# Softmax sums added up in the first key tile's buffer, one pool of eight PSUM banks, and weight splits shared between ScalarE and GpSimd

## The chip, the cores and the metric

The kernel is one launch on one core of a Trainium2 chip. The metric is device microseconds of one execution. Five engines have queues of their own and meet through semaphores: TensorE (PE in the profile, its weight loads PEld), VectorE (DVE), ScalarE (ACT), GpSimd (POOL) and SyncE (SP, which only issues DMAs). A wait stands in an engine's queue, so that everything behind a waiting instruction waits too.

## The reference, cut to what matters

Two layers over x of shape (2, 1024, 128), each with a residual:

```python
x = x + layernorm(attention(layernorm(x)))
x = x + layernorm(experts(layernorm(x)))

# attention: 8 query heads, 2 key heads (4 query heads each), causal
q = x @ wq
k = (x @ wk_down) @ wk_up
v = (x @ wv_down) @ wv_up
probs = softmax(mask(q k^T / sqrt(128)))      # exp / sum of exp
y = (probs @ v) @ wo

# experts: 32 routed (6 taken per token), one shared, 16 anchors (1 taken)
eo = (silu(x @ w_gate) * (x @ w_up)) @ w_down
```

## The kernel before, in words

**Tiling.** The 2048 rows are four chunks of 512 (two per batch). Attention runs over eight blocks n = 0 to 7, each one chunk of queries and one key head with its four query heads. Blocks 0, 1, 6 and 7 have four key tiles of 128 keys, blocks 2 to 5 have eight. Keys past the diagonal are left out, so the last four tiles of a block are 512, 384, 256 and 128 query columns wide.

**A block's steps.** `p1` (L1333, with the mask at L1336) multiplies queries by keys, and VectorE takes each row's maximum (`max`, L1095). The maxima, transposed (L1343), go by DMA into the rows below the queries. `p2` (L1354, mask L1356) multiplies again, the other way round and with the maximum subtracted, and ScalarE writes the exponentials of one key tile (four heads, 128x512 each) into `probs` (`exp`, L940), a ring of four buffers. `pv` (L1368) multiplies them by the values into the fixed PSUM bank `acc`. For the softmax's denominator, GpSimd adds each odd key tile into the even one before it, in two instructions of two heads (`add`, L759); `ones` (L1378) then multiplies the even tile by a column of ones, into the fixed PSUM bank `total`, once per pair of tiles. VectorE turns `total` into a reciprocal (`recip`, L1112 to L1114) and scales `acc` by it (`yl`, L1121). The `p1` of block n + 1 is laid between the `p2` of block n.

**After attention** each chunk goes through a projection (`post_out`, L1388), two normalisations and the routing, and then through 21 tiles of expert weights: three products `g` and three `u` (L1240 to L1242: each fp32 product is three products of rounded parts, high by high, low by high and high by low), `silu` (L971), a product with the routing weight on GpSimd (`mul`, L839), `h` (L1167), its high and low parts `hi` (L981) and `lo` (L1172), and `down` (L1439 to L1441) into the bank `acc`.

**The expert weights** are split into the same two parts during attention, in 22 pieces of at most 128x384: GpSimd writes the high part (L785, L790) and subtracts it (L786, L791).

**The order.** A planner (`Order.settle`) simulates the engines with the costs and ranks that `plan` gives each step, always starting the step that can start first (by rank if several can), and so writes every engine's queue and deals out six rotating PSUM banks. The order is fixed before the launch; on the chip only semaphores decide when each instruction starts. `bank_turn` makes TensorE wait until the bank's last reader is done.

Of the kernel before, what the change touches and what calls it, by code (L numbers as in the profile page):

```python
# [13 lines left out]
P = 128  # L14
# [34 lines left out]
BANKS = 6  # L49
KTBUF = 4  # L50
QRING = 3
HRING = 3
WSPLITS = range(0, MT, 3)
# [58 lines left out]
def halves_of(ev):  # L112

    return {j // 2 for j in range(ev[3], ev[3] + ev[4])}
# [5 lines left out]
ROUTE_RANK = (5.5, 100, 121, 142)  # L120
# [80 lines left out]
def plan():  # L201
# [7 lines left out]

    step("SP", ("x_load",), 320, 0)  # L210
# [5 lines left out]
    step("PE", ("warm",), 560, 0)  # L216
# [18 lines left out]
    step("PE", ("hold",), 130, 0.5, ("xT", 0))  # L235
# [33 lines left out]
    for n in range(NB):  # L269
# [25 lines left out]
        for x, ev in enumerate(steps):  # L295
# [5 lines left out]
            old = KT[n, kt] - KTBUF  # L301
            done = None
            if old >= 0:
                on, okt = KT_AT[old]
                done = ("ones", on, okt) if okt % 2 == 0 else ("add", on, okt, 1)
            step("ACT", ("exp", *ev[1:]), 22 + w * own * 80 // 1000, rank, ev, old >= 0 and ("pv", *KT_AT[old]), done)
            if ev == [e for e in steps if e[2] == kt][-1]:
                exps = [("exp", *e[1:]) for e in steps if e[2] == kt]
                step("PE", ("pv", n, kt), 10 + cols * 17 // 100, rank - 0.2, *exps, *vs,
                     ("pv", n, kt - 1) if kt else n >= 1 and ("yl", n - 1))  # L310
# [6 lines left out]
        step("DVE", ("recip", n), 170, n + 2, ("ones", n, kts(n) - 2))  # L317
# [30 lines left out]
    for a in range(3):  # L348
        step("SP", ("load", a), 200, 2, ("s_dma", 0) if a == 0 else ("wsplit", a - 1, WSPLITS[-1]))
        for t in WSPLITS:  # L350
            step("POOL", ("wsplit", a, t), 155, 3 + 2 * a + t / MT, ("wsplit", a, t - 3) if t else ("load", a), ("k_dma", NCH - 1) if a == 2 and t == 0 else None)

    last_exp = ("exp", *p2_steps(NB - 1)[-1][1:])
    for k in range(NU):
        m, t = divmod(k, MT)
        rank = 100 + k
        need = [("post_T_lo", m)] + ([("wsplit", 2, WSPLITS[-1]), last_exp] if k == 0 else [])
        if t != SHARED:
            step("PE", ("g", k), 68, rank, *need, k >= 1 and (("g", k - 1) if (k - 1) % MT != SHARED else ("u", k - 1)), bank=1, until=("silu", k))
# [22 lines left out]
    for half in range(2):  # L382
        step("ACT", ("tail_copy", half), 38, rank, ("down", NU - 1), ("fin_T", NCH - 2), half and ("tail_copy", 0))
        step("PE", ("tail_T", half), 27, rank, ("tail_copy", half), ("yl", NB - 1), bank=1 - half, until=("tail_center", half))
# [8 lines left out]
KT_AT = [(n, kt) for n in range(NB) for kt in range(kts(n))]  # L393
KT = {at: k for k, at in enumerate(KT_AT)}
# [28 lines left out]
ADD = count("POOL", "add")  # L423
MUL = count("POOL", "mul")
WSPLIT = count("POOL", "wsplit")
# [11 lines left out]
def build(nc, x, wq, small, wo, gate_bias, w_gate, w_up, w_down,  # L437
          shared_w_gate, shared_w_up, shared_w_down, anchor_w_gate, anchor_w_up, anchor_w_down, out):
    with ExitStack() as ctx:
# [94 lines left out]
        acc = ctx.enter_context(nc.psum_tensor("acc", [P, CH], F32))  # L534
        total = ctx.enter_context(nc.psum_tensor("total", [P, CH], F32))
# [57 lines left out]
        added = sem("added")  # L593
# [3 lines left out]
        route_done = sem("route_done")  # L597
        split_done = sem("split_done")
# [23 lines left out]
        def _(sp):  # L622
# [6 lines left out]
            for ev in PLAN["SP"]:  # L629
# [7 lines left out]
                elif kind == "load":  # L637
# [50 lines left out]
        def _(pool):  # L688
# [13 lines left out]
            for ev in PLAN["POOL"]:  # L702
# [805 lines left out]
```

## Time and profile before

| | |
|---|---|
| median of 3 runs | 416.88 us (416.11 to 418.38) |
| the profiled execution's own time | 416.28 us |
| its span in the trace | 414.2 us (2.1 us lie around it) |
| mean granted TensorE clock | 0.986 |
| TensorE matmul busy | 393.9 us, 95% of the span |
| VectorE busy | 281.5 us, 68% |
| GpSimd busy | 275.7 us, 67% |
| ScalarE busy | 231.4 us, 56% |

A matmul's busy time is modelled and overlaps with that of its neighbours, so what a matmul costs TensorE is read from the distance between starts, not from its duration. Attention proper lies between about 48 and 222 us of the span, the experts from there to 403 us, the tail behind.

### The profile page before, as it was taken

The page shows a single profiled execution, that of the slowest core. Times are in us where ns is not written, and L with a number is a line of the kernel's source. Part 1 is how long each engine was busy: PE and PEld are TensorE (multiplying, and loading weights), DVE is VectorE, ACT ScalarE, POOL GpSimd, SP SyncE. Part 2 cuts the span into 40 slices and gives each one's busy share as a digit, 9 for nine tenths or more (in the row PEclk, how much of TensorE's full clock was granted, in tenths as well). Part 3 has the DMA queues.
Part 4 walks back from the last instruction along what each step waited for, and adds up shares of the span by engine and source line. Part 5 has one row for each costly group of instructions (what it writes and reads, how often), then busy time and mean ns, then how long its engine had stood idle before and what let it go on. Part 6 is the DMA issues. An engine that isn't in the chain of part 4 may idle for free.

```text
span 414.2 us, 7003 instructions
## 1 busy us (share of the span) xinstructions
PE 393.9 (95%) x2168; PEld 260.5 (63%) x2168; DVE 281.5 (68%) x711; ACT 231.4 (56%) x450; POOL 275.7 (67%) x338
## 2 busy tenths in 40 slices
PE   8998999998999999999998999999999999999993
PEld 8664555553454644444556778767887788778871
DVE  5985897882857885526347776678765686557665
ACT  4555355564545466664675455865556655665643
POOL 6124867975976498473667886498963988477651
PEclk9989999998999999999999999999999999999997
DMA  7347090083230050500000000001000000000000
GB/s 215 52 108 169 16 220 13 0 196 52 40 38 3 2 77 3 71 9 2 3 0 2 1 1 2 0 0 28 1 1 2 25 2 0 1 2 25 0 2 25
DMA packets 9906, 14.56 MB, mean 35 GB/s; under 512 B 1232, under 2 KB 5520, under 8 KB 9488
## 3 DMA queue, kind: packets, MB, share of 16 engines
q1 hardware_dynamic: 9584, 13.49, 15.7%
q10 hardware_dynamic: 288, 0.64, 0.5%
q8 instruction: 19, 0.31, 0.4%
q14 instruction: 15, 0.12, 0.1%
HBM read 6.26 MB, written 1.05 MB: 18 GB/s over the span
## 4 chain that ended last, share of the span: by engine, by line
PE 77%; POOL 7%; DVE 6%; ACT 4%; issue 3%; DMA 2%; SPq 1%; POOLq 0%; DVEq 0%; ACTq 0%
PE ps L1240 9%; PE ps L1242 9%; PE ps L1241 9%; PE ps L1354 9%; PE ps L1333 9%; PE acc L1368 8%; PE total L1378 5%; PE acc L1439 4%; PE acc L1441 4%; PE acc L1440 4%; POOL silu L839 3%; DMA qst<-q_lo 2%; PE ps L1336 2%; PE ps L1356 1%; PE ps L1388 1%
## 5 line engine op out<-in xcount | busy, mean ns | idle before, releaser
L839 POOL TENSOR_TENSOR silu<-silu,cwb 128x512 f32<-128x512 f32 x80 | 102.5, 1292 | 40.3 <-ACT silu L971 35.8
L1095 DVE TENSOR_REDUCE nmax_h<-ps 128x1 f32<-128x512 f32 (+3 forms) x152 | 92.3, 655 | 47.8 <-PE ps L1336 24.3
L940 ACT ACTIVATE probs<-ps 128x512 f32<-128x512 f32 (+1 forms) x152 | 80.0, 579 | 70.2 <-PE ps L1354 43.7
L759 POOL TENSOR_TENSOR probs<-probs 128x768 f32<-128x768 f32 (+2 forms) x48 | 78.0, 1644 | 34.0 <-ACT probs L940 21.2
L1172 DVE TENSOR_TENSOR h_lo<-ps,h_hi 128x512 fp32r<-128x512 f32 (+1 forms) x84 | 57.0, 686 | 23.8 <-ACT h_hi L981 23.2
L1167 DVE TENSOR_TENSOR ps<-silu,ps 128x512 f32<-128x512 f32 (+1 forms) x84 | 57.9, 693 | 22.3 <-POOL silu L839 17.5
L971 ACT ACTIVATE silu<-ps 128x512 f32<-128x512 f32 x80 | 47.5, 597 | 45.5 <-PE ps L1242 39.7
L1333 PE MATMUL ps<-kst,qst 96*128 96x512 f32 (+3 forms) x192 | 63.8, 386 | 4.0 <-ACT probs L940 1.9
L1240 PE MATMUL ps<-xT_hi,w_hi 128*128 128x512 f32 x164 | 65.4, 399 | 1.3 <-ACT silu L971 1.3
L1242 PE MATMUL ps<-xT_hi,w_lo 128*128 128x512 f32 x164 | 64.4, 393 | 0.0
L1241 PE MATMUL ps<-xT_lo,w_hi 128*128 128x512 f32 x164 | 64.4, 393 | 0.0
L1354 PE MATMUL ps<-qst,kst 98*128 98x512 f32 (+1 forms) x152 | 62.4, 445 | 1.9 <-ACT probs L940 1.4
L981 ACT ACTIVATE h_hi<-ps 128x512 fp32r<-128x512 f32 (+1 forms) x84 | 49.8, 596 | 21.9 <-DVE ps L1167 20.9
L1333 PEld LDWEIGHTS ps<-kst,qst 96*128 96x128 f32 x192 | 34.0, 191 | 26.2 <-issue 21.1
L1354 PEld LDWEIGHTS ps<-qst,kst 98*128 98x128 f32 x152 | 27.9, 192 | 24.5 <-issue 21.9
L1368 PE MATMUL acc<-probs,v_sb 128*32 128x512 f32 (+3 forms) x384 | 40.4, 507 | 1.3 <-DVE ylat L1121 0.5
L1240 PEld LDWEIGHTS ps<-xT_hi,w_hi 128*128 128x128 f32 x164 | 30.8, 188 | 11.6 <-ACT silu L971 2.5
L1439 PE MATMUL acc<-h_hi,wd_hi 128*128 128x512 f32 (+1 forms) x84 | 35.0, 417 | 2.5 <-DVE h_lo L1172 2.4
L1242 PEld LDWEIGHTS ps<-xT_hi,w_lo 128*128 128x128 f32 x164 | 30.8, 188 | 6.8
L1241 PEld LDWEIGHTS ps<-xT_lo,w_hi 128*128 128x128 f32 x164 | 30.8, 188 | 6.7
L1441 PE MATMUL acc<-h_hi,wd_lo 128*128 128x512 f32 (+1 forms) x84 | 33.2, 395 | 0.0
L1440 PE MATMUL acc<-h_lo,wd_hi 128*128 128x512 f32 (+1 forms) x84 | 33.2, 395 | 0.0
(191 smaller groups left out, 518.7 us busy)
## 6 DMA issues: line engine op xcount, KB each, us to landing
qst<-q_hi SPq DMA_DIRECT2D x14, 256.0 KB, 5.6
qst<-q_lo SPq DMA_DIRECT2D x7, 256.0 KB, 6.1
x_sb<-in_attn_x SPq DMA_DIRECT2D x4, 256.0 KB, 6.5
raw<-in_ffn_w_gate SPq DMA_DIRECT2D x1, 1024.0 KB, 4.9
raw<-in_ffn_w_up SPq DMA_DIRECT2D x1, 1024.0 KB, 6.4
raw<-in_ffn_w_down SPq DMA_DIRECT2D x1, 1024.0 KB, 5.0
kst<-k_hi SPq DMA_DIRECT2D x6, 128.0 KB, 3.7
result<-x_sb SPq DMA_DIRECT2D x3, 256.0 KB, 2.3
```

What stands on the lines that cost most here:

```text
L759: nc.gpsimd.tensor_tensor(into, into, probs[:, k % KTBUF, js, cols], ALU.add).then_inc(added, 1)
L839: nc.gpsimd.tensor_tensor(silu[:, k % HRING, :], silu[:, k % HRING, :], cwb[:, m % 2, t // ET, :], ALU.mult).then_inc(scaled_ready, 1)
L940: nc.scalar.activation(probs[:, k % KTBUF, j:j + w, at:at + cols], bank(full)[:, 0:w * cols].rearrange("p (w c) -> p w c", w=w), ACT.Exp). ...
L1095: nc.vector.tensor_reduce(nmax_h[:, n % 2, i, j:j + w, h], bank(full)[:, 0:w * keys].rearrange("p (w k) -> p w k", w=w), AX.X, ALU.max, ne ...
L1167: nc.vector.tensor_tensor(up, silu[0:rows, k % HRING, :], up, ALU.mult).then_inc(h_ready, 1)
L1172: nc.vector.tensor_tensor(h_lo[0:rows, k % HRING, :], bank(("u", k))[0:rows], h_hi[0:rows, k % HRING, :].bitcast(F32), ALU.subtract).then_ ...
L1240: nc.tensor.matmul(dst, lhs[0], rhs[0], start=True, stop=False)
L1241: nc.tensor.matmul(dst, lhs[0], rhs[1], start=False, stop=False)
L1242: return nc.tensor.matmul(dst, lhs[1], rhs[0], start=False, stop=True)
L1333: last = nc.tensor.matmul(s[:, r, :], qst[0:QROWS, n % QRING, j + r, P * i:P * i + P], kst[0:QROWS, g, at:at + keys], start=(r == 0), stop ...
L1354: last = nc.tensor.matmul(s, kst[0:KROWS, g, at:at + P], qst[0:KROWS, n % QRING, j:j + w, first:first + cols], start=True, stop=not masked)
L1368: last = nc.tensor.matmul(acc[LAT * j:LAT * j + LAT, cols], v_sb[:, (T // P) * b + kt, LAT * g:LAT * g + LAT], probs[:, KT[n, kt] % KTBUF, ...
```

## The change

**Denominator.** All key tiles of a block are now added into the buffer of its first tile (kt = 0), one after the other, and `ones` runs once per block, at its end. An `add` is two instructions side by side: GpSimd takes the first two or three heads and VectorE the rest (`SPLIT`). So a block of eight tiles has seven adds on each of the two engines where GpSimd had four tiles' worth in eight instructions. The first tile's buffer is held to the end of the block, and three buffers rotate.

**Banks.** `acc` and `total` are gone. All eight PSUM banks rotate, and `pv`, `ones`, `down`, the warm-up products and the tail take theirs from the pool.

**Weights.** ScalarE writes the high parts (`whi`), GpSimd only subtracts. The down weights go from the last tiles to the first, because the first tiles of `wd_hi` lie over `k_hi` and `k_lo`, from which the last k transfer reads: only those wait for it.

**Transition.** The experts' buffers lie over `probs`. `silu`, `hi` and `lo` of the first three tiles now wait only for the reads of the one `probs` buffer under them (`rows_left`), instead of for all `pv` and `ones`.

```diff
-BANKS = 6
+BANKS = 8
 KTBUF = 4
+ADDERS = ("POOL", "DVE")
+SPLIT = (2, 3, 3, 3, 3, 3, 2, 2)
-WSPLITS = range(0, MT, 3)
+WSPLITS = [list(range(0, MT, 3)), list(range(0, MT, 3)), list(range(0, MT, 3))[::-1]]
+OVER_K = 2 * CH // P
-ROUTE_RANK = (5.5, 100, 121, 142)
+ROUTE_RANK = (5.5, 98, 121, 142)
...
+def part_heads(n, part):
+    return (SPLIT[n], REP) if part else (0, SPLIT[n])
...
-            step("ACT", ("exp", *ev[1:]), 22 + w * own * 80 // 1000, rank, ev, old >= 0 and ("pv", *KT_AT[old]), done)
+            step("ACT", ("exp", *ev[1:]), 22 + w * own * 80 // 1000, rank, ev, *leaves(WAS[n, kt]))
...
-                if kt % 2:
-                    for half in range(2):
-                        step("POOL", ("add", n, kt, half), 2 * (8 + cols * 252 // 1000), rank - 0.1, ("pv", n, kt - 1),
-                             *[e for e in exps if half in halves_of(e)])
-                    step("PE", ("ones", n, kt - 1), 10 + (CH - first_col(n, kt - 1)) * 17 // 100, rank - 0.2, ("add", n, kt, 0), ("add", n, kt, 1),
-                     ("ones", n, kt - 3) if kt > 1 else n >= 1 and ("recip", n - 1))
+                for part, engine in enumerate(ADDERS):
+                    if kt:
+                        j, end = part_heads(n, part)
+                        cost = 18 + (end - j) * cols * 215 // 1000 if engine == "POOL" else 15 + (end - j) * cols * 105 // 1000
+                        step(engine, ("add", n, kt, part), cost, rank - 0.1, ("pv", n, 0), *[e for e in exps if part in parts_of(e)], kt > 1 and ("add", n, kt - 1, part))
+        step("PE", ("ones", n), 10 + CH * 17 // 100, n + 2.9, *(("add", n, kts(n) - 1, part) for part in range(len(ADDERS))), bank=1, until=("recip", n))
...
+            step("ACT", ("whi", a, t), 55, 3 + 2 * a + i / len(WSPLITS[a]), ("load", a), i and ("whi", a, WSPLITS[a][i - 1]), a == 2 and t < OVER_K and ("k_dma", NCH - 1))
+            step("POOL", ("wsplit", a, t), 103, 3 + 2 * a + i / len(WSPLITS[a]), ("whi", a, t), before)
...
+        def rows_left(engine, row):
+            kt = (1, 2, 3, 0)[row // REP]
+            engine.wait_ge(pv_done, PV["pv", NB - 1, kt])
+            for part in range(len(ADDERS)):
+                engine.wait_ge(added[part], ADD[part]["add", NB - 1, kt, part])
...
+                elif kind == "add":
+                    _, n, kt, part = ev
+                    j, end = part_heads(n, part)
+                    cols = slice(first_col(n, kt), CH)
+                    into = probs[:, BUF[n, 0], j:end, cols]
+                    dve.wait_ge(pv_done, PV["pv", n, 0])
+                    dve.wait_ge(exp_ready, max(EXP["exp", *e[1:]] for e in p2_steps(n) if e[2] == kt and part in parts_of(e)))
+                    if kt > 1:
+                        dve.wait_ge(added[part], ADD[part]["add", n, kt - 1, part])
+                    nc.vector.tensor_tensor(into, into, probs[:, BUF[n, kt], j:end, cols], ALU.add).then_inc(added[part], 1)
```

Two places show how the queues move. VectorE before, in the `p1` of block 4, with block 3 being added up on GpSimd (L1095 is `max`, L1089 and L1081 are low parts of a projection and of a transposed chunk):

```order
L1121 TENSOR_TENSOR ylat<-acc,rb 128x512
L1095 TENSOR_REDUCE nmax_h<-ps 128x1
L1095 TENSOR_REDUCE nmax_h<-ps 128x2
L1089 TENSOR_TENSOR q_lo<-ps,q_hi 128x512
L1095 TENSOR_REDUCE nmax_h<-ps 128x2
L1095 TENSOR_REDUCE nmax_h<-ps 128x1 x9
L1081 TENSOR_TENSOR xT_lo<-ps,xT_hi 128x512
L1095 TENSOR_REDUCE nmax_h<-ps 128x1 x4
```

VectorE at the same place in the changed kernel (L1143 is `max`, L1137 and L1129 the same low parts, L1166 the `add` of one head):

```order
L1179 TENSOR_TENSOR ylat<-ps,rb 128x512
L1143 TENSOR_REDUCE nmax_h<-ps 128x2
L1137 TENSOR_TENSOR q_lo<-ps,q_hi 128x512
L1143 TENSOR_REDUCE nmax_h<-ps 128x2
L1166 TENSOR_TENSOR probs<-probs 128x512
L1143 TENSOR_REDUCE nmax_h<-ps 128x1 x3
L1166 TENSOR_TENSOR probs<-probs 128x512
L1143 TENSOR_REDUCE nmax_h<-ps 128x1 x6
L1129 TENSOR_TENSOR xT_lo<-ps,xT_hi 128x512
L1166 TENSOR_TENSOR probs<-probs 128x512
L1143 TENSOR_REDUCE nmax_h<-ps 128x1 x6
```

The adds stand among the maxima, one per key tile: three to six maxima lie between two of them. TensorE before, at the end of block 3 (L1368 is `pv`, L1333 and L1336 are `p1` of block 5, L1378 is `ones`):

```order
L1333 MATMUL ps<-kst,qst 128x512 x2
L1368 MATMUL acc<-probs,v_sb 32x256 x4
L1368 MATMUL acc<-probs,v_sb 32x128 x4
L1333 MATMUL ps<-kst,qst 128x128 x4
L1336 MATMUL ps<-mask,ident_bf 128x512
L1378 MATMUL total<-probs,ones 32x512 x4
L1378 MATMUL total<-probs,ones 32x256 x4
```

TensorE at the same place in the changed kernel (L1435 is `pv`, L1401 and L1404 are `p1` of block 5, L1422 is `p2` of block 4):

```order
L1401 MATMUL ps<-kst,qst 128x512 x2
L1435 MATMUL ps<-probs,v_sb 32x256 x4
L1435 MATMUL ps<-probs,v_sb 32x128 x4
L1401 MATMUL ps<-kst,qst 128x128 x4
L1404 MATMUL ps<-mask,ident_bf 128x512
L1422 MATMUL ps<-qst,kst 128x512 x2
```

Both `ones` groups are gone from here, and the block's single one stands eight rows further on, among the `p2` of block 4. Over the whole queue there are 8 groups of `ones` instead of 24 (16 of 512 columns and 8 of 256).

## Rows read from the trace of the kernel before

**Rows 1.** The page, parts 1 and 2: busy times, forty slices of the span.

```profile
PE 393.9 (95%) x2168; PEld 260.5 (63%) x2168; DVE 281.5 (68%) x711; ACT 231.4 (56%) x450; POOL 275.7 (67%) x338
...
PEclk9989999998999999999999999999999999999997
```

**Rows 2.** Busy time by stage: stretch, its length, each engine's busy us (instructions), clock.

```profile
48.50:222.50 174.00, 169.04 (x1090) 87.16 (x1091) 113.27 (x286) 97.50 (x195) 121.12 (x133) 0.99 0.24 44
222.50:403.40 180.90, 177.80 (x791) 140.74 (x789) 126.39 (x313) 106.96 (x201) 132.12 (x159) 1.00 0.02 5
```

**Rows 3.** The same by block, PE, PEld, DVE, ACT, POOL: blocks 1 to 5.

```profile
48.50:72.70 24.20, 23.13 (x135) 12.75 (x135) 21.09 (x40) 12.04 (x24) 17.73 (x23) 1.00 0.49 105
72.70:110.50 37.80, 35.91 (x218) 18.92 (x218) 24.84 (x56) 19.66 (x42) 29.39 (x33) 0.95 0.32 68
110.50:139.10 28.60, 28.14 (x182) 13.64 (x182) 20.27 (x54) 14.88 (x29) 20.49 (x23) 1.00 0.20 29
139.10:172.30 33.20, 32.43 (x207) 16.72 (x206) 23.71 (x74) 21.95 (x47) 22.47 (x27) 1.00 0.20 33
172.30:194.60 22.30, 22.21 (x157) 10.02 (x157) 9.80 (x18) 11.57 (x24) 14.39 (x8) 1.00 0.22 27
```

**Rows 4.** Waits: who waited for whom, us in total, times, longest.

```profile
DVE nmax_h L1095 <- PE ps L1336: 24.3, 19, 3.5
DVE nmax_h L1095 <- PE ps L1333: 23.1, 17, 5.3
```

**Rows 5.** Timeline, TensorE alone, around two `ones` groups: start, duration, instruction.

```profile
216.07 0.39 PE L1241 MATMUL ps<-xT_lo,w_hi 128*128 128x512 f32 x1
216.30 0.40 PE L1242 MATMUL ps<-xT_hi,w_lo 128*128 128x512 f32 x1
216.63 1.06 PE L1378 MATMUL total<-probs,ones 128*32 128x512 f32 x8
217.62 0.50 PE L1240 MATMUL ps<-xT_hi,w_hi 128*128 128x512 f32 x1
217.96 0.39 PE L1241 MATMUL ps<-xT_lo,w_hi 128*128 128x512 f32 x1
218.19 0.40 PE L1242 MATMUL ps<-xT_hi,w_lo 128*128 128x512 f32 x1
218.52 0.64 PE L1378 MATMUL total<-probs,ones 128*32 128x256 f32 x8
219.09 0.50 PE L1240 MATMUL ps<-xT_hi,w_hi 128*128 128x512 f32 x1
219.42 0.39 PE L1241 MATMUL ps<-xT_lo,w_hi 128*128 128x512 f32 x1
```

**Rows 6.** Groups by form: GpSimd's adds, a ScalarE exponential; busy us, mean ns, idle before.

```profile
L759 POOL TENSOR_TENSOR probs<-probs 128x1024 f32<-128x1024 f32 x16 | 37.8, 2378 | 8.2 <-PE acc L1368 6.6 <-ACT probs L940 1.6
L759 POOL TENSOR_TENSOR probs<-probs 128x256 f32<-128x256 f32 x16 | 11.3, 729 | 4.2 <-PE acc L1368 4.2
L940 ACT ACTIVATE probs<-ps 128x384 f32<-128x384 f32 x32 | 14.8, 491 | 9.0 <-PE ps L1354 8.7
```

**Rows 7.** Groups by line: GpSimd's high parts of the weights.

```profile
L785 POOL CAST w_hi<-raw 128x384 fp32r<-128x384 f32 (+1 forms) x14 | 6.9, 494 | 1.9 <-DMA raw<-in_ffn_anchor_w_up 1.9
L790 POOL CAST wd_hi<-raw 128x384 fp32r<-128x384 f32 (+2 forms) x8 | 3.7, 459 | 6.9 <-DMA kst<-k_lo 6.9
```

**Rows 8.** Page, part 5: a VectorE instruction with two inputs, one in PSUM.

```profile
L1172 DVE TENSOR_TENSOR h_lo<-ps,h_hi 128x512 fp32r<-128x512 f32 (+1 forms) x84 | 57.0, 686 | 23.8 <-ACT h_hi L981 23.2
```

**Rows 9.** The four instructions of line 1142: shortest, median and longest ns.

```profile
L1142 DVE TENSOR_TENSOR ties<-gscore x4: 216/217/1308, 129.7 to 322.4; 128x64 f32<-128x64 f32 x4
```

**Rows 10.** Timeline, VectorE and GpSimd, where both read SBUF.

```profile
276.60 1.29 POOL L839 TENSOR_TENSOR silu<-silu,cwb 128x512 f32<-128x512 f32 x1
277.10 0.87 DVE L1141 TENSOR_TENSOR above<-gscore 128x64 f32<-128x64 f32 x1
277.85 1.27 POOL L767 TENSOR_TENSOR x_sb<-x_sb,normed_x 128x512 f32<-128x512 f32 x1
277.89 1.31 DVE L1142 TENSOR_TENSOR ties<-gscore 128x64 f32<-128x64 f32 x1
```

**Rows 11.** Timeline around the transition; in brackets the idle time ahead.

```profile
219.26 1.28 ACT L971 ACT_TABLE_LOAD   x1 [3.04 <-PE total L1378]
...
221.20 0.50 PE L1240 MATMUL ps<-xT_hi,w_hi 128*128 128x512 f32 x1 [0.46 <-ACT silu L971]
```

**Rows 12.** Page, part 5: TensorE's two products of scores, with their idle time.

```profile
L1333 PE MATMUL ps<-kst,qst 96*128 96x512 f32 (+3 forms) x192 | 63.8, 386 | 4.0 <-ACT probs L940 1.9
...
L1354 PE MATMUL ps<-qst,kst 98*128 98x512 f32 (+1 forms) x152 | 62.4, 445 | 1.9 <-ACT probs L940 1.4
```

More of the change, by code:

```diff
@@ L109, in p2_steps, with parts_of, buffers @@
     return out
-def halves_of(ev):
-    return {j // 2 for j in range(ev[3], ev[3] + ev[4])}
+def part_heads(n, part):
+    return (SPLIT[n], REP) if part else (0, SPLIT[n])
+def parts_of(ev):
+    return {part for part in range(len(ADDERS)) if ev[3] < part_heads(ev[1], part)[1] and part_heads(ev[1], part)[0] < ev[3] + ev[4]}
+def buffers():
+    held, at, was = [None] * KTBUF, {}, {}
+    turn = list(range(KTBUF))
+    for n in range(NB):
+        for kt in range(kts(n)):
+            own = turn.pop(0)
+            if kt == 0:
+                first = own
+            else:
+                turn.append(own)
+            at[n, kt], was[n, kt], held[own] = own, held[own], (n, kt)
+        turn.append(first)
+    name = {at[NB - 1, kt]: k for k, kt in enumerate((1, 2, 3, 0))}
+    return {x: name[own] for x, own in at.items()}, was
 WARM = 14
@@ L208, in chunk_of, with leaves @@
         return CPB * b + c
+    def leaves(user, parts=range(len(ADDERS))):
+        if user is None:
+            return []
+        n, kt = user
+        return [("pv", n, kt), *(("add", n, kt, part) for part in parts)] if kt else [("ones", n)]
     step("SP", ("x_load",), 320, 0)
@@ L390, in plan @@
     return o, o.settle()
-KT_AT = [(n, kt) for n in range(NB) for kt in range(kts(n))]
-KT = {at: k for k, at in enumerate(KT_AT)}
+BUF, WAS = buffers()
 PLACED, PLAN = plan()
@@ L422 @@
 RSTD = count("POOL", "xn_rstd", "post_rstd", "post_rstd2", "fin_rstd")
-ADD = count("POOL", "add")
+ADD = [{ev: k + 1 for k, ev in enumerate(e for e in PLAN[engine] if e[0] == "add" and e[3] == part)} for part, engine in enumerate(ADDERS)]
 MUL = count("POOL", "mul")
-WSPLIT = count("POOL", "wsplit")
+W_HI = count("ACT", "whi")
 LN = {ev: k for k, ev in enumerate(MOM)}
@@ L592, in build @@
         pv_done = sem("pv_done")
-        added = sem("added")
+        added = [sem(f"added{part}") for part in range(len(ADDERS))]
         ones_done = sem("ones_done")
@@ L1371, in _ @@
                 elif kind == "ones":
-                    _, n, kt = ev
-                    cols = slice(first_col(n, kt), CH)
-                    pe.wait_ge(added, max(ADD["add", n, kt + 1, part] for part in range(2)))
-                    if kt == 0 and n >= 1:
-                        pe.wait_ge(recip_ready, n)
+                    n = ev[1]
+                    for part in range(len(ADDERS)):
+                        pe.wait_ge(added[part], ADD[part]["add", n, kts(n) - 1, part])
+                    bank_turn(ev)
                     for j in range(REP):
-                        last = nc.tensor.matmul(total[LAT * j:LAT * j + LAT, cols], ones[:], probs[:, KT[n, kt] % KTBUF, j, cols],
-                                                start=(kt == 0), stop=(kt == kts(n) - 2))
+                        last = nc.tensor.matmul(bank(ev)[LAT * j:LAT * j + LAT, :], ones[:], probs[:, BUF[n, 0], j, :], start=True, stop=True)
                     last.then_inc(ones_done, 1)
@@ L1418, in _ @@
                     if k == 0:
-                        pe.wait_ge(split_done, 3 * len(WSPLITS))
+                        pe.wait_ge(split_done, sum(len(order) for order in WSPLITS))
                     bank_turn(ev)
```

168 lines of the change are left out of this document (87 added, 81 removed).

## The prediction

> **What bounds the kernel now.** I read the page first, then the busy time by stage, then by block, then single instructions where a stage gains or loses. On the page TensorE is busy for 95% of the span, VectorE for 68%, GpSimd for 67%, ScalarE for 56% [rows 1]. By stage: TensorE is busy for 169.0 of the 174.0 us of attention and for 177.8 of the 180.9 us of the experts [rows 2]. So TensorE sets the pace in both, the experts' products are not touched, and the change can win or lose only in attention and at the seam behind it. By block the second engine is close: VectorE is busy for 21.1 of 24.2 us in block 1, and for 24.8 of 37.8, 20.3 of 28.6 and 23.7 of 33.2 us in blocks 2 to 4; GpSimd for 29.4, 20.5 and 22.5 us there [rows 3]. VectorE's free time is mostly a wait for scores from TensorE, 24.3 + 23.1 us over the span [rows 4]. That is what I expect to matter: the change takes work off the first engine and puts it on the second and the third.
>
> **What goes: `ones`.** The cost to TensorE is read from starts, since matmuls overlap. From the start of the L1242 product at 216.30 to that of the L1241 at 217.96 are 1.66 us; two steps between such products without `ones` are 2 x 0.23 (216.07 to 216.30); so a group of 512 columns costs 1.20 us. In the same way 218.19 to 219.42 is 1.23, less 0.46, gives 0.77 us for 256 columns [rows 5]. Before there are 16 wide and 8 narrow groups, after it 8 wide: 8 x 1.20 + 8 x 0.77 = 15.8 us less for TensorE, 3.2 us in each block of eight key tiles (3 x 1.20 + 0.77 - 1.20) and 0.8 in each of the four short ones.
>
> **What is added on GpSimd.** Its adds take 2378 ns for 1024 columns and 729 for 256 [rows 6]: 2.15 ns per column and 0.18 us. Three heads of 512 columns are then an estimated 3.48 us, and a long block (four tiles of 512 columns, then 384, 256, 128) costs 4 x 3.48 + 2.65 + 1.83 + 1.00 = 19.4 us, where it now costs 4 x 2.38 + 2 x 1.82 + 2 x 0.73 = 14.6: 4.8 us more. The short blocks fall slightly or stay. The high parts of the weights leave it, 6.9 + 3.7 = 10.6 us in all [rows 7], some 2 us of it in each of blocks 2 and 3.
>
> **What is added on ScalarE.** 22 copies of up to 128x384, by the 384-column exponential's 0.49 us [rows 6] 10.8 us, beside its 97.5 busy of 174 [rows 2]: nothing. A copy that waits for a weight load now holds the exponentials behind it, and TensorE's `pv` behind those. GpSimd waited 1.9 us for w_up and 6.9 for the k transfer ahead of the down weights [rows 4, 7]; the reversed order puts the tiles that do not need the transfer first. I take 0, with 5 us as the upper end (6.9 less the 1.9 that lie beside other work).
>
> **What is added on VectorE.** No SBUF-to-SBUF add of this size is in the trace. Between the 0.69 us of a 512-column subtraction with one input in PSUM [rows 8] and the 0.217 us median of 64 columns with both in SBUF [rows 9] lie 1.05 ns per column. So a long block costs 4 x 0.69 + 0.55 + 0.42 + 0.28 = 4.0 us, a short one at most 2.1.
>
> **The two adders in each other's way.** This is the term that decides. At 277.10 VectorE starts L1141, 64 columns with both inputs in SBUF, while GpSimd's product runs from 276.60 to 277.89. It takes 0.87 us and ends at 277.97. The next, L1142, starts at 277.89, GpSimd's L767 runs from 277.85 to 279.12, and it takes 1.31 us, to 279.20 [rows 10]. The median of the same instruction is 0.217 us [rows 9]. Each time VectorE ended 0.08 us behind GpSimd: it stood until the other had finished. GpSimd lost nothing (1.27 and 1.29 us). The new adds are just such instructions, on both engines at once.
>
> The Trainium skill says the same against this change (SBUF — State Buffer, Who interferes with whom): a VectorE instruction with two SBUF inputs takes its second through the read port that GpSimd uses, and whichever starts second stands until the first has ended, however long that is. The trace agrees, by those two rows. Without the rule and the rows the sum would be the 400 us of the second rival.
>
> How long is such a wait? GpSimd's adds in a long block have a mean remaining time, at a random moment in one, of (4 x 3.48² + 2.65² + 1.83² + 1.00²) / (2 x 19.4) = 1.55 us. GpSimd's needs in blocks 2 to 5 are 32.2, 23.3, 27.3 and 19.2 us (its busy time [rows 3], 4.8 more each, 2 less in the first two), 102 in all: 93% of the 109 us that TensorE would need there, 78% of the 131 that the sum below comes to. I take 85%, so 1.3 us per add and 9.1 per long block. From below it is 0. From above, VectorE's add becomes ready a head's exponential (0.6 us) after GpSimd's has started, and waits 2.5 us on the four wide tiles and 1 us on the others, 13 us per block.
>
> **The sum, block by block.** The longest of the three needs sets a block. VectorE's need is its busy time [rows 3] + 4.0 + 9.1.
>
> Block 2: VectorE 37.9 against TensorE 37.8 - 3.2 = 34.6; now 37.8, so +0.1. Block 3: VectorE 33.4 against 25.4; now 28.6, so +4.8. Block 4: VectorE 36.8 against 30.0; now 33.2, so +3.6. Block 5: VectorE 22.9; GpSimd 14.4 + 4.8 + 2.8 (its own turn behind seven VectorE adds) = 22.0; TensorE 19.1; now 22.3, so +0.6. Together +9.1.
>
> Block 1: VectorE 21.1 + 1.3 + three short waits, 1.2, is 23.6 against TensorE's 23.4; now 24.2, so -0.6. Blocks 0, 6 and 7 keep TensorE's -0.8 each, -2.4. At the seam ScalarE waited 3.04 us for the last `ones` before it loaded the table for silu, and TensorE then 0.46 us for silu [rows 11]; with the waits per buffer I take -1. The eight banks and the ranks: both products of scores together have 5.9 us of idle time ahead of them, most of it not for maxima [rows 12], so more banks are worth nothing here.
>
> Sum: 9.1 - 0.6 - 2.4 - 1 = +5.1 us on the profiled execution's 416.28, so 421.4, where the median of its runs is 416.88. I predict 421.
>
> **Bounds.** With no wait between the adders: block 2 to 4 by TensorE (-9.6), block 5 by GpSimd's 19.2 (-3.1), the others -4.2: 399.4. With the upper wait: VectorE 41.8, 37.3, 40.7 and 26.8 gives +24.7, the others -4.0: 437.0.
>
> **Rivals.**
> First, the waits are real but lie in time that VectorE has anyway. For it: 47.4 us of VectorE's idle time are waits for scores [rows 4], and in the sparse stretches behind a block's last maximum an add can stand without anyone waiting. Against it: VectorE's adds stand three to six maxima apart amid the `p1` of the next block, where TensorE needs the banks that the maxima free. If 0.5 us of each wait counts (3.5 per long block), VectorE's needs are 32.3, 27.8 and 31.2, so TensorE keeps block 2 (-3.2), and blocks 3 and 4 give -0.8 and -2.0, block 5 is -0.3 by GpSimd: with the -4.0, -10.3, so 406. I give 404 to 414 a chance of 0.29.
>
> Second, TensorE keeps the whole gain, as by its own work alone, the lower bound: 399 to 404. For it: TensorE is at 97% in attention [rows 2]. Against it: the waits of [rows 10]. Chance 0.09.
>
> Third, the worse side of my own mechanism: VectorE's add always comes just behind GpSimd's, and GpSimd itself, near full in blocks 3 to 5, delays the single `ones` at the block's end. It decides from about 2 us per wide add: above 429, up to 437. Chance 0.11.
>
> Fourth, gain and wait cancel, between 415 and 419. For it: both are of the same size, 15.8 against 9.1 per long block less VectorE's free time. Chance 0.13.
>
> That the change does not do what it says is excluded for `ones`: the queue has 8 groups. For the order of the down weights the price is the 0 to 5 us above.
>
> **How the numbers follow.** My forecast, VectorE bound by the waits at 419 to 429, has 0.38. A run of this kernel is told from no change at about 0.5%, 2.1 us. Slower: 0.38 + 0.11 = 0.49. Same: 0.13. Faster: 0.29 + 0.09 = 0.38. The range of 8 in 10 leaves out the lowest and the highest tenth: 404 to 431. The forecast's own range is 419 to 429.
>
> **What would show it.** TensorE's `ones` line: 64 records for 192, about 8 us of busy time for 21.9. VectorE's adds of 512 columns: a mean near 2 us, where 0.69 would refute the wait; GpSimd's 1536-column add near 3.5 us. VectorE's waits for scores should shrink from 47 us to under 20, and TensorE should wait in blocks 2 to 4 for maxima (`nmax_h`), which it hardly does now [rows 12]. Blocks 3 and 4 should be longer than 28.6 and 33.2 us, the experts' 181 us unchanged. I am wrong if the VectorE adds run at 0.7 us, or if they take 2 us and blocks 2 to 4 are still shorter than before.

## The result, and the profile after

The changed kernel takes 442.38 us (median of 4 runs, 439.23 to 445.77), where the kernel before took 416.5 beside it (415.19 to 418.38). The ratio is 1.062, with a 95% interval of 1.053 to 1.071. The forecast of 421 had the sign right. The time lies 11 us above the top of its range. The profiled execution took 442.87 us, 440.8 of them its span.

The page after, parts 1 and 2, answers to [rows 1]:

```profile
PE 402.0 (91%) x2040; PEld 267.2 (61%) x2040; DVE 352.7 (80%) x751; ACT 241.3 (55%) x472; POOL 288.5 (65%) x308
...
PEclk9999979898986596989699999999999999999999
```

VectorE is 71 us busier. TensorE runs 128 records fewer and is 8 us busier all the same: the clock row has holes in attention where it had none to speak of before, and the records last longer at the lower clock (blocks 1 to 5 under `reduce`: 158.3 for 135.7 us with the same 819). The experts are as before: from 267 to 430 us TensorE is busy for 161.2 of 163.0.

The blocks after, answering to [rows 3], blocks 1 to 5 and then 6 and 7 (stretch, length, PE, PEld, DVE, ACT, POOL, granted clock, DMA):

```profile
44.60:72.00 27.40, 24.61 (x125) 14.14 (x124) 24.88 (x41) 12.61 (x26) 14.11 (x12) 0.88 0.43 94
72.00:115.40 43.40, 37.04 (x204) 20.27 (x205) 40.02 (x66) 25.43 (x54) 31.06 (x23) 0.92 0.28 59
115.40:158.50 43.10, 36.90 (x168) 18.57 (x167) 38.16 (x60) 16.64 (x31) 22.03 (x11) 0.72 0.13 19
158.50:196.80 38.30, 32.76 (x176) 16.86 (x176) 35.83 (x57) 18.53 (x36) 26.68 (x22) 0.87 0.24 35
196.80:227.10 30.30, 27.01 (x151) 12.11 (x151) 25.81 (x51) 15.75 (x32) 23.73 (x15) 0.89 0.08 11
227.10:238.00 10.90, 10.50 (x76) 5.96 (x74) 7.77 (x21) 6.42 (x16) 6.96 (x11) 1.00 0.01 3
238.00:249.50 11.50, 10.65 (x76) 6.02 (x76) 8.96 (x33) 7.96 (x16) 8.26 (x11) 1.00 0.00 1
```

A block ends where VectorE scales its `pv` (`yl`). Blocks 1 to 5 are 3.4, 5.6, 14.5, 5.1 and 8.0 us longer than before (by the same ends of blocks: 24.0, 37.8, 28.6, 33.2, 22.3). Blocks 0, 6 and 7 are 3.4, 4.2 and 1.3 shorter. That makes 27.7 by the end of the last block, and the span is 26.6 longer. Block 5 also holds 33 VectorE instructions more than before (51 for 18): its seven adds, six maxima more (block 6 has seven fewer), and some 20 short ones, mostly of the routing, that ran in block 4 before.

The adds and `ones` after, by form (busy us, mean ns, idle before), answering to [rows 6]:

```profile
L807 POOL TENSOR_TENSOR probs<-probs 128x1536 f32<-128x1536 f32 x16 | 56.4, 3522 | 26.0 <-ACT probs L987 19.4 <-issue 4.3 <-PE ps L1435 2.0
L1166 DVE TENSOR_TENSOR probs<-probs 128x512 f32<-128x512 f32 x19 | 46.7, 2460 | 1.2 <-ACT probs L987 0.6 <-issue 0.4
...
L1444 PE MATMUL ps<-probs,ones 128*32 128x512 f32 x64 | 8.8, 619 | 1.0 <-POOL probs L807 0.8 <-DVE nmax_h L1143 0.2
```

VectorE's wide add takes 2460 ns, where 512 columns with one input in PSUM take 693. One of them, with GpSimd beside it, answering to [rows 10]:

```profile
78.48 3.82 DVE L1166 TENSOR_TENSOR probs<-probs 128x512 f32<-128x512 f32 x1
...
78.29 3.46 POOL L807 TENSOR_TENSOR probs<-probs 128x1536 f32<-128x1536 f32 x1
```

GpSimd's ends at 81.75, VectorE's at 82.30: it stood for 3.3 us and ran on for 0.55 us. At 104.17 GpSimd is idle, and an add of 384 columns takes 0.54. So what one add costs hangs on where GpSimd is when it comes.

The waits (who waited for whom, us in total, times, longest), answering to [rows 4]:

```profile
PE ps L1401 <- DVE nmax_h L1143: 9.0, 9, 2.1
...
DVE nmax_h L1143 <- PE ps L1404: 5.8, 10, 2.4
DVE nmax_h L1143 <- PE ps L1401: 5.5, 9, 1.9
PE ps L1422 <- DVE nmax_h L1143: 5.1, 3, 2.4
```

They have turned round: VectorE waited 47.4 us for scores, now 11.3, and TensorE waits 14.1 us for maxima.

### The profile page after: what moved, and what is told of

It reads as the page before. It is cut to its first block, busy times and chain, and to the rows that moved or that the text cites. A ratio compares the mean times of both kernels' runs of the same rounds, so it can differ in the third digit from the quotient of the medians.

```text
span 440.8 us, 6951 instructions
## 1 busy us (share of the span) xinstructions
PE 402.0 (91%) x2040; PEld 267.2 (61%) x2040; DVE 352.7 (80%) x751; ACT 241.3 (55%) x472; POOL 288.5 (65%) x308
## 4 chain that ended last, share of the span: by engine, by line
PE 45%; DVE 8%; POOL 3%; issue 3%; ACT 2%; POOLq 0%; ACTq 0%; DVEq 0%
PE ps L1308 8%; PE ps L1309 8%; PE ps L1310 8%; PE ps L1502 5%; PE ps L1504 4%; PE ps L1503 4%; DVE probs L1166 2%; PE ps L1422 2%; DVE nmax_h L1143 2%; PE ps L1435 2%; PE ps L1401 2%; POOL probs L807 1%; ACT probs L987 1%; POOL silu L874 1%; DVE h_lo L1232 1%
## 5 line engine op out<-in xcount | busy, mean ns | idle before, releaser
L807 POOL TENSOR_TENSOR probs<-probs 128x1536 f32<-128x1536 f32 (+5 forms) x40 | 97.7, 2444 | 60.9 <-ACT probs L987 45.3
L1143 DVE TENSOR_REDUCE nmax_h<-ps 128x1 f32<-128x512 f32 (+3 forms) x152 | 92.2, 650 | 11.4 <-PE ps L1404 5.8
L1401 PE MATMUL ps<-kst,qst 96*128 96x512 f32 (+3 forms) x192 | 71.4, 431 | 12.4 <-DVE nmax_h L1143 9.0
L1422 PE MATMUL ps<-qst,kst 98*128 98x512 f32 (+1 forms) x152 | 68.5, 487 | 6.5 <-DVE nmax_h L1143 5.1
L1166 DVE TENSOR_TENSOR probs<-probs 128x512 f32<-128x512 f32 (+4 forms) x40 | 67.5, 1688 | 5.2 <-ACT probs L987 3.1
L1017 ACT ACTIVATE silu<-ps 128x512 f32<-128x512 f32 x80 | 47.4, 597 | 43.2 <-PE ps L1310 37.7
L1401 PEld LDWEIGHTS ps<-kst,qst 96*128 96x128 f32 x192 | 39.3, 219 | 32.6 <-issue 27.9
L1422 PEld LDWEIGHTS ps<-qst,kst 98*128 98x128 f32 x152 | 31.3, 215 | 32.4 <-issue 30.5
L1435 PE MATMUL ps<-probs,v_sb 128*32 128x512 f32 (+3 forms) x384 | 46.1, 567 | 0.5 <-ACT probs L987 0.5
L1502 PE MATMUL ps<-h_hi,wd_hi 128*128 128x512 f32 (+1 forms) x84 | 34.7, 414 | 3.3 <-DVE h_lo L1232 3.2
L1503 PE MATMUL ps<-h_lo,wd_hi 128*128 128x512 f32 (+1 forms) x84 | 33.2, 395 | 0.0
```

The source lines that it names most:

```text
L807: nc.gpsimd.tensor_tensor(into, into, probs[:, BUF[n, kt], j:end, cols], ALU.add).then_inc(added[part], 1)
L1143: nc.vector.tensor_reduce(nmax_h[:, n % 2, i, j:j + w, h], bank(full)[:, 0:w * keys].rearrange("p (w k) -> p w k", w=w), AX.X, ALU.max, ne ...
L1166: nc.vector.tensor_tensor(into, into, probs[:, BUF[n, kt], j:end, cols], ALU.add).then_inc(added[part], 1)
L1401: last = nc.tensor.matmul(s[:, r, :], qst[0:QROWS, n % QRING, j + r, P * i:P * i + P], kst[0:QROWS, g, at:at + keys], start=(r == 0), stop ...
L1422: last = nc.tensor.matmul(s, kst[0:KROWS, g, at:at + P], qst[0:KROWS, n % QRING, j:j + w, first:first + cols], start=True, stop=not masked)
```

## The experiments

All of them start from the changed kernel. Theory A: VectorE's adds stand behind GpSimd's because both their inputs are in SBUF, and this standing is the loss. Its rivals: the adds' own work, the place in the queue or the planner's order (B), and, later, TensorE's lowered clock as a loss in its own right (C).

**reduce.**

```
- nc.vector.tensor_tensor(into, into, probs[:, BUF[n, kt], j:end, cols], ALU.add)
+ nc.vector.tensor_reduce(spare[:, kt - 1, j:end], probs[:, BUF[n, kt], j:end, cols], AX.X, ALU.max)
```

> The changed kernel, with each add on VectorE replaced by a reduction over the same heads and columns (one SBUF input; VectorE's share of the denominators is left out). Same queues, same work on VectorE, no second SBUF input. Theory A (VectorE stands while GpSimd reads SBUF, and that stop spreads to TensorE and its clock): the reductions take about 0.69 us instead of 2.46, TensorE is at the lower clock for under 15 us instead of 58, and the time is 398 to 408 us. Theory B (the 20 us of extra work on VectorE, or the held buffer and the single ones at the end of a block, are what costs): still above 430 us, with reductions at 0.69 us.

Measured: 404.53 us (403.73 to 405.18), 0.968 of the kernel before (0.964 to 0.971).

```profile
L1167 DVE TENSOR_REDUCE spare<-probs 128x1 f32<-128x512 f32 x16 | 10.9, 680 | 2.6 <-ACT probs L988 1.5 <-issue 1.2
```

The same tile, place in the queue and waits, but one SBUF input, and the instruction takes 680 ns while GpSimd adds beside it. That is 38 us off the changed kernel. B is out as an explanation of the loss. One detail missed: with a mean clock of 0.975 over 401.7 us TensorE spent an estimated 20 us at half clock, where under 15 were expected. Its blocks 1 to 5:

```profile
44.00:66.70 22.70, 21.25 (x126) 12.07 (x126) 21.93 (x42) 12.55 (x26) 12.37 (x11) 1.00 0.48 112
66.70:105.50 38.80, 35.08 (x205) 19.31 (x205) 31.04 (x65) 25.21 (x54) 30.13 (x24) 0.91 0.33 67
105.50:132.80 27.30, 26.80 (x168) 14.18 (x168) 25.85 (x60) 16.30 (x31) 21.25 (x11) 1.00 0.21 31
132.80:164.80 32.00, 29.30 (x176) 15.84 (x175) 26.84 (x58) 18.33 (x36) 25.45 (x21) 0.95 0.28 42
164.80:188.80 24.00, 23.31 (x151) 10.83 (x149) 19.51 (x51) 15.33 (x32) 22.57 (x17) 1.00 0.11 14
```

This is the table that gives the size. In the changed kernel VectorE is busier in these blocks by 2.9, 9.0, 12.3, 9.0 and 6.3 us, 39.5 together, and the blocks are longer by 4.7, 4.6, 15.8, 6.3 and 6.3, 37.7 together. Nearly every microsecond that VectorE is busier by is a microsecond of the kernel. Blocks 1 to 5 as one stretch, first in the changed kernel, then in `reduce`:

```profile
44.60:227.10 182.50, 158.32 (x819) 81.95 (x818) 164.70 (x271) 88.96 (x178) 117.60 (x83) 0.85 0.23 42
...
44.00:188.80 144.80, 135.73 (x819) 72.23 (x818) 125.18 (x272) 87.72 (x178) 111.76 (x82) 0.96 0.29 53
```

VectorE is idle for 17.8 us there in the one and for 19.6 in the other. The standing did not go into its idle time; it came on top.

**one_column.**

```
- nc.vector.tensor_tensor(into, into, probs[:, BUF[n, kt], j:end, cols], ALU.add)
+ few = probs[:, BUF[n, 0], j:end, CH - 1:CH]
+ nc.vector.tensor_tensor(few, few, probs[:, BUF[n, kt], j:end, CH - 1:CH], ALU.add)
```

> The changed kernel, with each add on VectorE cut to one column of its heads (the rest of VectorE's share of the denominators is left out). VectorE keeps two SBUF inputs but has hardly any work. Theory A: each such add still ends when GpSimd's instruction does, so it takes 1 to 2 us on the wide tiles in place of 0.16, and the time stays at 425 to 440 us. Theory B: the time falls to 400 to 410 us.

Measured: 428.11 us (425.83 to 429.22), 1.023 of before (1.017 to 1.028).

```profile
L1167 DVE TENSOR_TENSOR probs<-probs 128x1 f32<-128x1 f32 x31 | 44.3, 1431 | 4.1 <-ACT probs L987 4.0
```

One column with two SBUF inputs takes twice as long as 512 columns with one, and a kernel with almost no adding work on VectorE is 24 us slower than `reduce`, which reads the whole tile. So the standing costs without the work, as A says. Its blocks 1 to 5:

```profile
44.10:213.50 169.40, 149.46 (x820) 76.65 (x819) 150.33 (x272) 89.12 (x178) 112.26 (x83) 0.91 0.25 45
```

Against `reduce` VectorE is 25.2 us busier there and the blocks are 24.6 longer. But the changed kernel, where the adds stand about as long and do their work besides, is busier by another 14.4 us and longer by another 13.1. So beside the standing the work of the adds is paid as well; VectorE's idle time is again about the same, 19.1 us.

**per_head.**

```
- nc.gpsimd.tensor_tensor(into, into, probs[:, BUF[n, kt], j:end, cols], ALU.add)
+ for h in range(j, end):
+     one = probs[:, BUF[n, 0], h, cols]
+     last = nc.gpsimd.tensor_tensor(one, one, probs[:, BUF[n, kt], h, cols], ALU.add)
```

> The changed kernel, with GpSimd's add cut into one instruction per head (512 columns, 1.28 us, instead of 1536 columns, 3.52 us); VectorE unchanged, result complete. Theory A: VectorE's wait ends with GpSimd's current instruction, so its 512-column add falls from 2.46 us to 1.2 to 1.5 us, and the time to 408 to 425 us, though GpSimd issues some 8 us more. Theory B: GpSimd has more to do and the time is 442 us or more.

Measured: 425.52 us (423.81 to 425.96), 1.018 of before (1.014 to 1.022), half a microsecond above the 408 to 425 that A gave.

```profile
L1169 DVE TENSOR_TENSOR probs<-probs 128x512 f32<-128x512 f32 x19 | 21.7, 1140 | 1.5 <-issue 0.9 <-ACT probs L990 0.2
...
L1447 PE MATMUL ps<-probs,ones 128*32 128x512 f32 x64 | 11.1, 775 | 5.7 <-POOL probs L809 5.4 <-DVE nmax_h L1146 0.3
```

With GpSimd's instruction cut to a third, VectorE's wide add falls from 2460 to 1140 ns and the time by 17 us. The wait goes with the length of GpSimd's single instruction, as A says (it gave 1.2 to 1.5 us for the add). In return GpSimd is 15 us busier (303.8 for 288.5), and `ones` at the blocks' ends now waits 5.4 us for it.

**psum_sum.** VectorE has one head in every block; its sum lies in a fixed PSUM bank, seven banks rotate (and the planner's cost of the last add is 80 higher, for the copy back).

```
- SPLIT = (2, 3, 3, 3, 3, 3, 2, 2)
+ SPLIT = (3,) * 8
- BANKS = 8
+ BANKS = 7
+ if kt == 1: last = tensor_tensor(dsum[:, cols], into[:, 0, :], probs[:, BUF[n, kt], j, cols], ALU.add)
+ else:       last = tensor_tensor(dsum[:, cols], dsum[:, cols], probs[:, BUF[n, kt], j, cols], ALU.add)
+ (after the last tile)  tensor_copy(probs[:, BUF[n, 0], j, whole], dsum[:, whole])
```

> The changed kernel with VectorE's share (one head in every block) summed in a PSUM bank of its own: all its adds but the first of a block have one SBUF input, and a copy back to SBUF closes a block; seven banks rotate. Result complete. Theory A: only the 8 first adds can stand, and the time is 400 to 412 us, faster than the kernel before. Theory B: 435 us or more, since VectorE has 4 us more to do in copies.

Measured: 436.2 us (431.09 to 436.43), 1.039 of before (1.031 to 1.048): A's forecast missed by 24 us.

```profile
L1170 DVE TENSOR_TENSOR dsum<-probs 128x512 f32<-128x512 f32 x4 | 13.0, 3240 | 0.0
...
L1172 DVE TENSOR_TENSOR dsum<-dsum,probs 128x512 f32<-128x512 f32 x12 | 8.3, 692 | 1.9 <-issue 1.8
```

The mechanism holds within one kernel: with `dsum` as an input 692 ns, with both inputs in SBUF 3240. I had left one of the latter in each block, and in the four long ones it ran into a GpSimd add of 1536 columns (in the four short ones, with 384 columns, it took 1182 ns). Whether that, the bank that is gone or the new split made the rest, this run alone can't say. The next two were made to tell.

**seven_banks.** The edit is `BANKS = 8` to `7` in the changed kernel, the control.

> The changed kernel with seven PSUM banks in the rotation in place of eight, nothing else; the control for psum_sum and for filler. If the missing bank is what psum_sum paid for: 450 us or more, and the first block ends near 52 us as there. If a bank fewer is worth little: 440 to 447 us, first block ends within 2 us of the 45.3 us of the changed kernel.

Measured: 448.88 us (447.28 to 456.93), 1.079 of before (1.070 to 1.088); the same kernel again, as `seven_again`, 451.18 (447.02 to 454.11), 1.076 (1.063 to 1.089). The numbers fall between the two cases: a bank costs 6.5 us, in the second pair 8.8, and most of it is in block 0, which ends at 51.0 us (50.0) for 45.3. Blocks 2 to 5 took 151.1 and 156.5 us, for 155.1 with eight banks: there a bank fewer shows no effect. So the forecast's step "more banks are worth nothing here" was wrong: it looked at the two products of scores and not at the first block.

> The kernel of seven_banks again, on the same chip as light_filler, as the other side of that comparison: 447 to 452 us, clock near 0.936.

**psum_copy.** As `psum_sum`, the split as in the changed kernel, and no VectorE add with two SBUF inputs in blocks 1 to 5 (the planner's costs for the copies are 69 each):

```
+ if kt == 1: link(nc.vector.tensor_copy(dsum[:], probs[:, BUF[n, 0], j, :]))
+ last = nc.vector.tensor_tensor(dsum[:, cols], dsum[:, cols], probs[:, BUF[n, kt], j, cols], ALU.add)
```

> Seven banks; in the five blocks where VectorE has one head (1 to 5), the sum of that head lies in the eighth bank: the first tile is copied there by VectorE, each later tile is added with one input in PSUM and one in SBUF, and the sum is copied back to the first tile's buffer. The first, seventh and eighth block are as in the changed kernel. Result complete. No VectorE instruction there reads two SBUF inputs. Theory A (VectorE's two-SBUF-input adds stand until GpSimd's instruction ends, and this is the loss): adds 0.7 us each, time 405 to 418 us, so equal to or better than the kernel before. Rival S (psum_sum was slow for the bank or the planner's order, not for its eight first adds): 430 us or more. Copies that read one SBUF input should take 0.7 us even while GpSimd adds.

Measured: 421.39 us (417.97 to 422.53), 1.012 of before (1.003 to 1.021).

```profile
L1173 DVE TENSOR_TENSOR dsum<-dsum,probs 128x512 f32<-128x512 f32 x16 | 11.1, 695 | 1.0 <-issue 0.8
...
L1172 DVE COPY dsum<-probs 128x512 f32<-128x512 f32 x5 | 3.4, 687 | 0.2 <-issue 0.2
```

Against its own control with seven banks it is 27.5 us faster, though VectorE runs ten instructions more. It is a few microseconds over the 418 that A gave; S (430 or more) is out. Block by block against `psum_sum`, the latter's eight first adds and split cost 2.3 us in block 0, 12.3 in blocks 1 to 5 and 4.8 in blocks 6 and 7, 19.4 in all, of which 15.8 are left at the end of the span. So its miss of 24 us was mostly in my edit: some 7 us are the bank's, some 15 these two together, and how those share it was not separated.

**psum_take.** All eight banks rotate; the sum's bank is handed out with one more TensorE instruction and comes back after the copy back.

```
+ step("PE", ("take", n), 60, rank - 0.2, *exps, ("pv", n, 0), bank=1, until=("add", n, kts(n) - 1, 1))
+ nc.tensor.matmul(bank(ev), ident[:], probs[:, BUF[n, 0], SPLIT[n], :], start=True, stop=True)
```

> As psum_copy, but all eight banks rotate: in blocks 1 to 5 the bank for VectorE's sum is taken from the rotation when TensorE copies the first tile's head there (one matmul with the identity, some 0.5 us), and given back after VectorE's copy back. Result complete. Theory A, and the first block's 5 us of psum_copy being the price of the missing bank: first block ends near 45 us, blocks 3 to 5 as in psum_copy, 412 to 418 us in all, so 0 to 1.5% below the kernel before. Rival: the bank held through a block costs as much as the missing one: 420 us or more.

Measured: 414.26 us (median of 6, 407.56 to 415.76), the kernel before 416.56 (median of 11, 412.83 to 421.53). Block 0 ends at 46.0 us, and the wide add takes 692 ns. The result is complete: the change with its fault mended. The medians are 0.6% apart and the runs overlap, so it is the kernel before or a little better, and no more can be said. Its block 2 takes 42.8 us for 37.8 before, at a granted clock of 0.88; why is open.

**casts_back.** The 22 roundings of the high parts go back to GpSimd: `step("POOL", ("whi", a, t), 55, ...)` and `nc.gpsimd.tensor_copy`.

> The changed kernel with the 22 roundings of the weights' high parts given back to GpSimd (some 0.75 us a tile), ahead of its subtractions. If the moved roundings cost nothing and bring GpSimd little within attention: 440 to 447 us, as the changed kernel. If GpSimd's time in attention is what sets the blocks: 450 us or more, since 22 times 0.75 to 1.4 us come back on it. If ScalarE's copies were in the way: below 438 us.

Measured: 439.66 us (439.28 to 443.49), 1.060 of before (1.051 to 1.069), against 1.062 with them on ScalarE. The move costs and brings nothing that shows.

**filler and light_filler.** Are the holes in the clock a loss of their own? TensorE gets one more 128-column product ahead of each second product of scores, in seven banks, so against `seven_banks`.

```
+ nc.tensor.matmul(idle[:, 0:P], ident[:], ident[:], start=True, stop=True)
  pe.wait_ge(shift_in[n % QRING], 16 * (n // QRING + 1))
```

> As seven_banks, with one more 128-column matmul of the identity, into a bank that nobody reads, queued ahead of each of the 152 second score passes, before that pass's wait. It adds TensorE work (at the full clock near 0.15 us each, some 20 us in all where TensorE is the bound), and keeps TensorE active just ahead of waits. Theory C (the waits draw the clock to half, and this makes half of the loss or more): the mean granted clock comes back toward 0.97 and the time rises by less than the 20 us, or falls: between 15 us below and 8 us above seven_banks. Theory W (the waits alone make the loss, the clock is a small part): time up by 10 us or more, whatever the clock.

> As filler, with the extra matmul in bf16 and so lighter on TensorE (near 0.06 us each, some 9 us in all, where the f32 one of filler took two records and near 0.14 us). It separates the clock from the price of the extra work. Theory C (the lowered clock carries a share of the loss that is worth several us): the mean granted clock rises to 0.96 or more and the time falls 4 to 15 us below seven_banks. Theory W (TensorE only waits for VectorE, at either clock): the time stays within 3 us of seven_banks or rises by up to 9 us, although the clock rises.

Measured: `filler` 453.16 us (448.4 to 455.09), clock 0.977 over the span for 0.936; `light_filler`, with `ident_bf`, 449.07 (445.14 to 452.19), clock 0.961, beside 451.18 and 0.923 for `seven_again`. By what was written down, `filler` (+4.3) spoke for C, and `light_filler` (-2.1, within 3) for W. Blocks 2 to 5 of `light_filler` and of `seven_again`:

```profile
74.90:226.90 152.00, 132.17 (x807) 67.85 (x805) 136.81 (x230) 77.40 (x150) 103.06 (x71) 0.92 0.19 34
```

```profile
76.40:232.90 156.50, 134.44 (x693) 68.64 (x693) 139.62 (x229) 76.46 (x151) 102.63 (x71) 0.85 0.17 29
```

The clock there goes from 0.85 to 0.92, and the stretch is 4.5 us shorter, 2.8 of which VectorE stood less. The control's own two profiles lie 5.4 us apart in these blocks (151.1 and 156.5), so this difference is not clear of noise.

Nor was the extra work as small as expected. From one first product of scores to the next, with a second product between them, lie 0.47 us of starts in the changed kernel:

```profile
126.20 0.40 PE L1401 MATMUL ps<-kst,qst 96*128 96x512 f32 x1
126.43 0.40 PE L1422 MATMUL ps<-qst,kst 98*128 98x512 f32 x1
126.67 0.40 PE L1401 MATMUL ps<-kst,qst 96*128 96x512 f32 x1
```

With the fillers, `light_filler` and then `filler`, it is 0.59 and 0.69 us, at the same durations of a product:

```profile
116.49 0.40 PE L1402 MATMUL ps<-kst,qst 96*128 96x512 f32 x1
...
117.08 0.40 PE L1402 MATMUL ps<-kst,qst 96*128 96x512 f32 x1
```

```profile
114.42 0.39 PE L1402 MATMUL ps<-kst,qst 96*128 96x512 f32 x1
...
115.11 0.40 PE L1402 MATMUL ps<-kst,qst 96*128 96x512 f32 x1
```

That is 0.12 and 0.22 us per filler, where 0.06 and 0.14 were expected, and an estimated 14 and 25 us of added work in blocks 2 to 5. The higher clock may have given back as much as this work took, so the two runs do not say what the clock alone is worth. A limit comes from VectorE's row: it was idle for 17.8 us in blocks 1 to 5 of the changed kernel, at a clock of 0.85, and for 19.6 in `reduce`, at 0.96. So the low clock brought VectorE no idle time that `reduce` does not have too, and with VectorE as busy as it was, a full clock could have won back no more than those 17.8 us. Whether it would have won any is open.

## Why the prediction was right in sign and wrong in size

**`ones`: right.** 64 records and 8.8 us of busy time, for 64 and about 8.

**GpSimd's adds: right.** 3522 ns for 1536 columns, for 3.48 us; 2698 for 1152 and 1944 for 768, for 2.65 and 1.83.

**ScalarE's copies at nothing: right**, by `casts_back`. The 503 ns of one were 0.49 in the forecast.

**The price of one add on VectorE without waits: right.** In PSUM form 692 to 695 ns, for 0.69.

**The wait between the adders: right in kind, and in size by its mean.** Forecast 9.1 us per long block and 1.2 in block 1, 37.6 in blocks 1 to 5 (four long blocks and the short one); measured against `reduce` 39.5. Over the 28 adds of the long blocks VectorE's line is busy for 53.6 us, for 15.8 in `reduce`: 1.35 us of standing per add, where I took 1.3. That mean hides a spread that the forecast did not have: the wide add stands 1.77 us (2460 less 693), the narrow ones about 0.4 to 0.7. The Trainium skill's rule (SBUF — State Buffer, Who interferes with whom) names exactly this pair, and that a VectorE instruction with at most one SBUF input escapes, outside the modes that use both of its ports. The runs agree with both: 1431 ns for one column with two SBUF inputs, 680 and 692 ns for 512 columns with one.

**"The longest of the three needs sets a block": the step that failed.** By it, 22.0 of the 37.6 us of standing reached the time (399.4 to 421.4), since the rest was to lie in VectorE's free time. In the runs 37.7 of 39.5 did, and 38 us of the kernel's time. The rule takes the engines as working side by side, each with a queue of work in front of it. Here they pass a few banks to and fro: TensorE writes scores, VectorE takes the maximum, and only then has TensorE the bank again. An add that stands for 2 to 3 us in VectorE's queue holds the maxima behind it; TensorE runs out of banks and waits (14.1 us); then VectorE waits for new scores (11.3 us, and by the windows it is idle for 15.3 us in blocks 2 to 5 although it is "the bound" there). Neither catches up what it lost. That the standing was paid in full is measured; that the hand-over of banks is the reason is read from these waits and was not put to a test of its own; one bank fewer showed no effect in blocks 2 to 5.

Where nothing stands the rule fares better only in the total, and by luck. `reduce` took 404.5 us, and the forecast's bound without waits was 399.4. But by that bound blocks 1 to 5 take 23.4, 34.6, 25.4, 30.0 and 19.2 us, 132.6 together, and in `reduce` they took 144.8: 12.2 more. Blocks 0, 6 and 7 made up for 8.1 of it (10.5 us shorter than before, where 2.4 were forecast). Part of both is the new order: TensorE has 78 records fewer in blocks 1 to 5 (897 before, 819 after), where the missing `ones` alone are 104, so some 26 of other work moved in. So of the 21 us by which I missed, some 16 are this step, and 4 to 5 the base, itself a difference of two larger errors. I had also treated the clock as constant; the page shows that it isn't, and what that cost is open.

**The block order: wrong in detail.** The forecast gave VectorE its old work in each block. The planner put 26 instructions besides the adds into block 5, and in `reduce` VectorE is busy there for 19.5 us, where the forecast had 9.8 + 4.0. Of the +8.0 us of block 5 (forecast +0.6), 6.3 are the standing and 1.7 the rest, by `reduce`. Blocks 6 and 7 gained 5.5 us, not 1.6. Block 0 gained 3.4 us, not 0.8; the eighth bank has its part in that, since with seven the block ends at 51.0 us, later than before.

**Rivals.** The first (waits in free time, 404 to 414) was the forecast's own fault carried further, and fell most clearly. The 47.4 us of waits for scores that spoke for it are also not most of VectorE's free time over the span, which is 132.7 us, but only of that in attention, 60.7. The second is `reduce`: what the change would do if VectorE's adds stood for nothing. The third, "worse side of my own mechanism", was the nearest with 429 to 437, but put its price on waits of over 2 us per wide add. They were 1.8. The price was in what a wait is worth. The fourth, gain and wait cancelling at 415 to 419, fell by the same step.

**What would show it.** All that was listed came out: adds near 2 us (2.46, and 985 to 1086 for the middle ones), waits for scores under 20 us, TensorE waiting for `nmax_h`, blocks 3 and 4 longer, the experts unchanged.

## What to carry to other kernels

Here two engines handed each other buffers in a fixed order, and a stall on one of them, 80 to 90% busy, was paid almost in full; where a kernel looks like this, count a stall whole until a trace shows that idle time took it up. Before an add is moved to VectorE beside a busy GpSimd, ask where its inputs lie: with one of them in PSUM it runs at its own speed, with both in SBUF it waited for what GpSimd had begun. And a bank or buffer that is freed or taken is to be priced in each stage, not only in the one that the change is about.

## What the runs showed of the hardware that I had not expected

Even the smallest VectorE instruction stands: one column took 1431 ns on average, and single ones 2.92 and 3.14 us, each ending 0.02 to 0.03 us behind a GpSimd add of 1536 columns that had begun 0.3 to 0.6 us before it:

```profile
149.35 2.92 DVE L1167 TENSOR_TENSOR probs<-probs 128x1 f32<-128x1 f32 x1 [0.24 <-ACT probs L987]
156.37 3.14 DVE L1167 TENSOR_TENSOR probs<-probs 128x1 f32<-128x1 f32 x1
```

```profile
148.80 3.45 POOL L807 TENSOR_TENSOR probs<-probs 128x1536 f32<-128x1536 f32 x1 [6.36 <-ACT probs L987]
156.04 3.44 POOL L807 TENSOR_TENSOR probs<-probs 128x1536 f32<-128x1536 f32 x1
```

Both adders wait for exponentials of the same tile, and these single ones came shortly after GpSimd's began. GpSimd loses little in return: 3522 ns beside VectorE's adds, 3475 without them. A VectorE copy of 512 columns from SBUF to PSUM did not stand: 687 ns on average, and 0.69 us where it began inside a GpSimd add (`psum_copy`):

```profile
117.22 3.48 POOL L808 TENSOR_TENSOR probs<-probs 128x1536 f32<-128x1536 f32 x1 [4.35 <-ACT probs L988]
117.76 0.69 DVE L1172 COPY dsum<-probs 128x512 f32<-128x512 f32 x1 [0.15 <-issue]
```

TensorE's clock was granted at 0.72 of full speed over block 3, so more than half of that block ran at 1.2 GHz, where TensorE waits for maxima (3.4 us of waits for `nmax_h`); in the same block of `reduce`, without the standing adds, it was 1.00.
